# Final normalization: ten sequences added to the output by accumulating transfers, six by VectorE, and no barrier ahead of it

## The reference

```python
x = x + _L1_xattn_ref(_layernorm(x, axis=-1), ctx_1024)        # "x3" in the kernel
x = x + _L1_ffn_ref(_layernorm(x, axis=-1), ...)
# and the end of _L1_ffn_ref, whose argument z is the normed x3:
out = jnp.einsum('bted,bte->btd', y, combine)                  # top-2 of 8 experts
return _layer_norm(z + out, gamma, beta)
# so the result is  x3 + (norm(z + out) * gamma + beta)
```

## Time and profile before

| | |
|---|---|
| median of 3 runs | 1369.33 us (1367.33 to 1369.45) |
| the profiled execution | 1379.14 us |
| its span | 1377.3 us |
| TensorE busy | 1145.9 us, 83% of the span |
| VectorE busy | 938.2 us, 68% |
| ScalarE busy | 799.8 us, 58% |
| GpSimd busy | 650.4 us, 47% |
| moved by transfers | 162.79 MB, mean 118 GB/s |

### The profile page before, as it was taken

One profiled execution on the slowest core, in us unless ns is written; L12 is line 12 of the kernel. 1 busy time (PEld: TensorE's weight loads), 2 busy tenths in 40 slices (PEclk: granted clock), 3 DMA queues, 4 the chain that ended last, 5 costly groups with the idle time before them and its releaser, 6 DMA issues.

```text
span 1377.3 us, 24047 instructions
## 1 busy us (share of the span) xinstructions
PE 1145.9 (83%) x8296; PEld 1052.9 (76%) x8296; DVE 938.2 (68%) x2066; ACT 799.8 (58%) x1579; POOL 650.4 (47%) x581
## 2 busy tenths in 40 slices
PE   3889899898859999999948560999999999999920
PEld 2688778787648888888837450999999999999920
DVE  6667877876436666666347564678878788787848
ACT  3745666552325565555436520777787877778724
POOL 3434443333235666665424664354554544545347
PEclk8559998899979999999978775899999999999965
DMA  6543333211065666666369990233332333333256
GB/s 224 167 164 112 137 122 120 108 54 39 24 209 166 176 175 174 176 172 180 48 200 266 229 194 11 54 59 52 56 55 52 59 52 55 55 52 59 39 158 223
DMA packets 142313, 162.79 MB, mean 118 GB/s; under 512 B 29457, under 2 KB 122897, under 8 KB 140145
## 3 DMA queue, kind: packets, MB, share of 16 engines
q1 hardware_dynamic: 113120, 124.97, 29.8%
q0 software_dynamic: 27968, 35.48, 15.5%
q10 hardware_dynamic: 1104, 0.82, 0.2%
HBM read 117.36 MB, written 43.86 MB: 117 GB/s over the span
## 4 chain that ended last, share of the span: by engine, by line
PE 62%; DVE 13%; DMA 7%; issue 7%; ACT 5%; POOL 4%; POOLq 1%; SPq 1%; ACTq 0%; DVEq 0%
PE quad L1929 15%; PE pb L1948 12%; PE quad L1191 11%; PE pb L1206 6%; PE pb L354 4%; PE quad L300 4%; DMA c3T<-in_ctxT 4%; PE pb L368 3%; POOL dSL L1803 2%; DVE Dm L522 1%; PE pb L266 1%; ACT Dm L838 1%; POOLq L2230 1%; PE pb L1176 1%; PE quad L1910 1%
## 5 line engine op out<-in xcount | busy, mean ns | idle before, releaser
L1993 DVE TENSOR_TENSOR wl<-W,wh 128x1024 fp32r<-128x1024 f32 x156 | 188.4, 1228 | 86.4 <-ACT gl L2068 57.6
L2100 POOL DMA_INDIRECT dOUT<-y,es x71 | 135.3, 1905 | 219.8 <-DVE y L2025 210.1
L1948 PE MATMUL pb<-wh,hh 128*128 128x256 f32 x568 | 164.0, 289 | 0.0
L1948 PE MATMUL pb<-wh,hl 128*128 128x256 f32 x568 | 160.5, 283 | 0.0
L1948 PE MATMUL pb<-wl,hh 128*128 128x256 f32 x568 | 160.5, 283 | 0.0
L1332 POOL DMA_INDIRECT dACC<-ye,idxJ x64 | 100.6, 1572 | 103.6 <-ACT ye L1295 54.4
L2042 ACT CAST wh<-W 128x1024 fp32r x117 | 121.9, 1049 | 41.0 <-issue 29.1
L2068 ACT ACTIVATE gl<-quad,b1c 128x256 f32<-128x256 f32 (+1 forms) x312 | 124.7, 450 | 20.0 <-PE quad L1929 18.7
L1929 PE MATMUL quad<-xh,wh 128*128 128x256 f32 (+1 forms) x624 | 126.1, 284 | 6.7 <-ACT hh L2073 5.2
L1929 PE MATMUL quad<-xh,wl 128*128 128x256 f32 (+1 forms) x624 | 125.6, 283 | 0.0
L1929 PE MATMUL quad<-xl,wh 128*128 128x256 f32 (+1 forms) x624 | 125.6, 283 | 0.0
(11 more groups left out here) (282 smaller groups left out, 3202.7 us busy)
## 6 DMA issues: line engine op xcount, KB each, us to landing
MB<-dM SPq DMA_DIRECT2D x16, 1024.0 KB, 5.7
W<-in_W SPq DMA_DIRECT2D x16, 1024.0 KB, 10.8
wraw<-in_Wg SPq DMA_DIRECT2D x16, 512.0 KB, 6.5
wraw<-in_Wu SPq DMA_DIRECT2D x16, 512.0 KB, 8.0
wraw<-in_Wd SPq DMA_DIRECT2D x16, 512.0 KB, 5.3
b2c<-in_b SPq DMA_DIRECT2D x39, 128.0 KB, 3.2
xp<-in_x SPq DMA_DIRECT2D x16, 256.0 KB, 5.5
cT<-in_ctxT SPq DMA_DIRECT2D x16, 256.0 KB, 5.2
```

The costliest lines, as they stand in the source:

```text
L1948: ins = pe.matmul(bank.t[:, 0:256], a_[s][:, c, 128 * tt:128 * tt + 128], b_[n % 3][:, 256 * c:256 * c + 256], start=half == 0 and m == 0, ...
L1993: v.tensor_tensor(w_dst(wl[n % 3], kind), w_src(expert(i), kind, half), w_dst(wh[n % 3], kind), ALU.subtract).then_inc(*v_t.up("w", n))
L2100: g.indirect_dma_start(out=dOUT[:, :], out_offset=bass.IndirectOffsetOnAxis(ap=es[i % 6][:, tt, 1:2].bitcast(U32), axis=0), in_=y1[i % 2][ ...
```

## The change

x3 is stored straight into the rows of the output, and `dX3` is gone. During stage 4, in visits 4 to 19, GpSimd adds beta to the output's rows, one sequence at a time, with an accumulating transfer from the broadcast tile `bet`; for this gamma and beta are loaded at the end of stage 3. The barrier between stages 4 and 5 is gone: SP waits for the last scatters (`sy_st`) before it loads z, and all other waits of stage 5 follow from its loads. Stage 5 works on pairs of sequences, 128 x 4 columns of statistics at once, all 16 z tiles stay in place, and there is no load of x for the first ten sequences: GpSimd adds their norm * gamma to the output's rows with accumulating transfers. For the last six SP loads the output's rows (x3 + beta), VectorE adds in place and SP stores. ScalarE may overwrite a tile of `nc_` (four pairs) when its accumulating transfer has landed.

```diff
@@ stage 3, SP
-                    sp.dma_start(by_chunk(dX3[pair_rows(j), :]), x2[j % 4][:, :, :]).then_inc(*x3_st[j % 4].up(j, by=16))
+                    sp.dma_start(by_chunk(out[pair_rows(j), :]), x2[j % 4][:, :, :]).then_inc(*x3_st[j % 4].up(j, by=16))
...
+            sp.dma_start(gam[:, :], to_all(A["gamma"], D)).then_inc(*ln_ld.up("g", by=16))
+            sp.dma_start(bet[:, :], to_all(A["beta"], D)).then_inc(*ln_ld.up("b", by=16))
+            for s in (w1_ld, w2_ld, ln_ld, *x3_st, *z_st):
@@ stage 4, GpSimd (the loads of gamma and beta leave SP's part)
                 if i + 3 < VISITS:
                     gather(i + 3)
+                if 0 <= i - 4 < B:
+                    g.dma_start(by_chunk(out[rows(i - 4), :]), bet[:, :].unsqueeze(1).to_broadcast([128, 2, D]), accum_op=ALU.add
+                                ).then_inc(*beta_st.up(i - 4, by=16))
...
             g.wait_ge(*sy_st.all())
+            g.wait_ge(*beta_st.all())
@@ stage 5, new
+        ADDED = 2 * (PAIRS - 3)
+            def stats(j):
+                s = fsm[j]
+                for c in range(4):
+                    if c % 2 == 0:
+                        v.wait_ge(*fz_ld[2 * j + c // 2].of())
+                    ins = v.bn_stats(s[:, c, 0:6], zc[j][:, c, :])
...
+            def scale(b):
+                n = nc_[b // 2 % 4][:, chunks(b), :]
                 v.wait_ge(*a_f.of("n", b))
+                v.tensor_tensor(n, n, gam[:, :].unsqueeze(1).to_broadcast([128, 2, D]), ALU.mult).then_inc(*v_f.up("g", b))
+                if b >= ADDED:
+                    v.wait_ge(*v_f.of("g", b))
+                    v.wait_ge(*fx_ld[(b - ADDED) // 2].all())
+                    v.tensor_tensor(n, n, xc[(b - ADDED) // 2][:, chunks(b), :], ALU.add).then_inc(*v_f.up("y", b))
+
+            for j in range(PAIRS + 1):
+                if j < PAIRS:
+                    stats(j)
+                if j == 1:
+                    v.wait_ge(*ln_ld.all())
+                if j:
+                    scale(2 * j - 2)
+                if j < PAIRS:
+                    shift(j)
+                if j:
+                    scale(2 * j - 1)
...
+        def act_stage5(a):
+            for j in range(PAIRS):
...
+                    if c % 2 == 0 and j >= 4:
+                        a.wait_ge(*out_ad[b % 8].of(b - 8))
...
+        def pool_stage5(g):
+            def add(b):
+                g.wait_ge(*v_f.of("g", b))
+                g.dma_start(by_chunk(out[rows(b), :]), nc_[b // 2 % 4][:, chunks(b), :], accum_op=ALU.add
+                            ).then_inc(*out_ad[b % 8].up(b, by=16))
+
+            for j in range(PAIRS):
+                s = fsm[j]
+                g.wait_ge(*v_f.of("v", j))
+                g.tensor_tensor(s[:, :, 8:9], s[:, :, 9:10], mhalf[:, :].unsqueeze(1).to_broadcast([128, 4, 1]), ALU.pow).then_inc(*g_f.up("r", j))
+                if 0 < j <= ADDED // 2:
+                    add(2 * j - 2)
+                    add(2 * j - 1)
...
+        def sp_stage5(sp):
+            sp.wait_ge(*sy_st.all())
             for b in range(B):
+                sp.dma_start(zc[b // 2][:, chunks(b), :], by_chunk(dOUT[rows(b), :])).then_inc(*fz_ld[b].up(by=16))
+            sp.wait_ge(*beta_st.all())
+            for b in range(ADDED, B):
+                sp.dma_start(xc[(b - ADDED) // 2][:, chunks(b), :], by_chunk(out[rows(b), :])).then_inc(*fx_ld[(b - ADDED) // 2].up(b, by=16))
+            for b in range(ADDED, B):
                 sp.wait_ge(*v_f.of("y", b))
+                sp.dma_start(by_chunk(out[rows(b), :]), nc_[b // 2 % 4][:, chunks(b), :]).then_inc(*out_st.up(b, by=16))
@@ the programs of all engines: a barrier after stages 1 to 3 only
-                if n < 4:
+                if n < 3:
                     end_of_stage(v, n + 1)
```

More of the change, by code:

```diff
@@ L2116, in sp_stage4 @@
                 sp.dma_start(b2c[i % 4][:, :], A["b2"][bass.ds(r, 1), :].to_broadcast([128, D])).then_inc(*b2_ld[i % 4].up(i, by=16))
-            sp.dma_start(gam[:, :], to_all(A["gamma"], D)).then_inc(*ln_ld.up("g", by=16))
-            sp.dma_start(bet[:, :], to_all(A["beta"], D)).then_inc(*ln_ld.up("b", by=16))
-            sp.wait_ge(*ln_ld.all())
         M7.st.close()
         M8 = Mem()
-        fsm = M8.ring("fsm", 4, [128, 2, 16])
-        zc = M8.ring("zc", 12, [128, 2, D])
-        xc = M8.ring("xc", 8, [128, 2, D])
@@ L2128, in build @@
[L2128 to L2132, removed]
+        fsm = M8.ring("fsm", PAIRS, [128, 4, 16])
+        zc = M8.ring("zc", PAIRS, [128, 4, D])
+        nc_ = M8.ring("nc", 4, [128, 4, D])
+        xc = M8.ring("xc", 3, [128, 4, D])
+        ADDED = 2 * (PAIRS - 3)
+        fz_ld, fx_ld = ring("moe_loaded", B), ring("x3_loaded", 3)
+        out_ad, out_st = ring("out_added", 8), sig("out_stored")
@@ L2133, in build @@
         v_f, a_f, g_f = sig("dve_final"), sig("act_final"), sig("pool_final")
-        def x3_of(b):
-            return xc[b % 8]
         def dve_stage5(v):
[L2140 to L2149, removed]
-                    ins = v.bn_aggr(s[:, c, 6:8], s[:, c, 0:6])
[L2151 to L2157, removed]
+            def stats(j):
[4 more added lines that the diff above has]
+                    ins = v.bn_stats(s[:, c, 0:6], zc[j][:, c, :])
+                ins.then_inc(*v_f.up("s", j))
+                v.wait_ge(*v_f.of("s", j))
+                for c in range(4):
+                    ins = v.bn_aggr(s[:, c, 6:8], s[:, c, 0:6])
+                ins.then_inc(*v_f.up("a", j))
+                v.wait_ge(*v_f.of("a", j))
+                v.tensor_scalar(s[:, :, 9:10], s[:, :, 7:8], EPS, None, ALU.add).then_inc(*v_f.up("v", j))
@@ L2158, in shift @@
+            def shift(j):
+                s = fsm[j]
+                v.wait_ge(*g_f.of("r", j))
                 v.scalar_tensor_tensor(out=s[:, :, 10:11], in0=s[:, :, 6:7], scalar=-1.0, in1=s[:, :, 8:9],
-                                       op0=ALU.mult, op1=ALU.mult).then_inc(*v_f.up("b", b))
+                                       op0=ALU.mult, op1=ALU.mult).then_inc(*v_f.up("b", j))
             def scale(b):
+                n = nc_[b // 2 % 4][:, chunks(b), :]
                 v.wait_ge(*a_f.of("n", b))
-                v.tensor_tensor(nc_[b % 4][:, :, :], nc_[b % 4][:, :, :], gam[:, :].unsqueeze(1).to_broadcast([128, 2, D]),
-                                ALU.mult).then_inc(*v_f.up("g", b))
@@ L2166, in total @@
[L2166 to L2181, removed]
@@ L2184, in act_stage5 @@
-        def act_stage5(a):
-            for b in range(B):
[L2186 to L2202, removed]
@@ new lines, in act_stage5 @@
+        def act_stage5(a):
+            for j in range(PAIRS):
+                s = fsm[j]
+                a.wait_ge(*v_f.of("b", j))
+                for c in range(4):
+                    b = 2 * j + c // 2
+                    if c % 2 == 0 and j >= 4:
+                        a.wait_ge(*out_ad[b % 8].of(b - 8))
+                    ins = a.activation(nc_[j % 4][:, c, :], zc[j][:, c, :], ACT.Identity, scale=s[:, c, 8:9], bias=s[:, c, 10:11])
+                    if c % 2:
+                        ins.then_inc(*a_f.up("n", b))
@@ L2219, in sp_stage5 @@
+        def sp_stage5(sp):
+            sp.wait_ge(*sy_st.all())
+            for b in range(B):
+                sp.dma_start(zc[b // 2][:, chunks(b), :], by_chunk(dOUT[rows(b), :])).then_inc(*fz_ld[b].up(by=16))
[3 more added lines that the diff above has]
+            for b in range(ADDED, B):
                 sp.wait_ge(*v_f.of("y", b))
-                sp.dma_start(by_chunk(out[rows(b), :]), yc[b % 4][:, :, :]).then_inc(*out_st[b % 4].up(b, by=16))
@@ L2221, in sp_stage5 @@
-            for s in out_st:
+                sp.dma_start(by_chunk(out[rows(b), :]), nc_[b // 2 % 4][:, chunks(b), :]).then_inc(*out_st.up(b, by=16))
+            for s in (*out_ad, out_st):
                 sp.wait_ge(*s.all())
@@ L2235, in tensor_program @@
                 stage(pe)
-                end_of_stage(pe, n + 1)
+                if n < 3:
+                    end_of_stage(pe, n + 1)
         def vector_program(v):
```

5 lines of the change are left out of this document (2 added, 3 removed).

## The result

The changed kernel runs in 1364.9 us (median of 19 runs), the kernel before in 1372.9 us (also 19): the ratio is 0.9941, 95% interval 0.9927 to 0.9955, so 8.1 us faster (6.2 to 10.0). Forecast were 6.7 us. The 19 runs of before scatter from 1367.3 to 1379.5, more widely than the three of the first table.

A forecast was written before the change was run, and what follows sets the result against it. The bound was taken as VectorE's order in the last stage, behind a start waiting for barrier and first loads. Terms gave -8.6 us, less 1.9 for GpSimd's issues: 1369.3 - 6.7 = 1362.6 us, range 1357.5 to 1370.5.

The forecast's parts named there:

- Barrier: Seam between stages four and five: SP issues its first load without waiting for GpSimd's drain, -4.4 us.
- First loads: Start of stage five: all z go first, so the second z lands after 4.6 us, not 6.35.
- Pitch: Stage five, pairs without x: 4.43 us each, with VectorE waiting for the same pair's power; five take 22.2 us.
- Pairs with x: Stage five, three pairs with x on VectorE: 5.5 us each for two, 2.7 for the last.
- GpSimd's issue: Stage five, ten accumulating transfers: issuing one takes a = 1.55 us, stretching five pitches to 4.81, adding 1.9 us.
- the threshold of 1.36: Stage five: issue time a above which GpSimd's cycle is longer than 4.43 us and each of five pitches grows.
- the cycle of 1.71 + 2a: GpSimd's time per pair in stage five: power 1.01, signal 0.1, two issues of a plus 0.30 gap each.
- Rival 1: Dearer issues make GpSimd pace stage five: +3.7 us at 2.59, +8.8 at 3.1; chances 7 and 7 in 100.
- The two ends: Extremes of issue time in stage five: a = 0.96 leaves -8.6 us, a = 3.1 gives +8.8.
- Landing: Last stage's additions: 256 rows take 1.95 us of all DMA engines; ten end near 1357, covered by 10 us.
- Rival 2: Additions land slowly in the last stage: one after another at 7.4 us each, +32 us; 10 in 100.
- Stage four: Sixteen beta transfers in stage four hide in GpSimd's waits for y, costing nothing; rival 0 to 16 us, 8 in 100.

The follow-up runs named there:

- e1: The changed kernel with the barrier ahead of the last stage put back; ratio to the kernel before 0.9955 (0.9935 to 0.9974).
- e2: The kernel before with only the last barrier replaced by SP's wait for the scatters; ratio to the kernel before 0.9977 (0.9956 to 0.9998).
- e4: The changed kernel with both scales ahead of the shift in VectorE's order; ratio to the kernel before 0.9916 (0.9890 to 0.9943).
- e5: The changed kernel with VectorE one pair further ahead and GpSimd's adds one iteration later; ratio to the kernel before 0.9890 (0.9859 to 0.9921).
- e8: The changed kernel with GpSimd's ten last-stage transfers storing instead of accumulating; ratio to the kernel before 0.9913 (0.9884 to 0.9942).
- e10: The changed kernel with fourteen sequences added by accumulating transfers and two by VectorE; ratio to the kernel before 0.9984, one run each.
- e9: The changed kernel with sixteen more beta transfers, in visits 20 to 35 of stage four; ratio to the kernel before 0.9942, one run each.

## Why the prediction was right

**Barrier, -4.4.** Right, by e1 (5.4 us put back) and e2 (4.3 taken out of the old kernel).

**First loads.** The forecast gain came and was larger by 1.2 us. Eps of the first pair was due 5.9 us after the first load and came after 4.7, because the second z landed 3.5 us after the first load, when VectorE wanted it, and not 4.6. How much of this is the order of loads is not shown: with the old order the second z came after 6.4 us (before) or 4.3 (e2).

**Pitch.** 4.43 was forecast, 4.22 measured. The stall was placed rightly and nearly to its size: from eps to shift 1.69 (1345.92 to 1347.61), forecast 1.70, with a power of 1.39, forecast 1.36. What was off is VectorE's own work, 1.84 for statistics and aggregation instead of 2.02. e4 and e5 show that this stall is the pace.

**Pairs with x.** 4.95 instead of 5.5: power and add did not queue on each other, the shift came after 1.69 us as before.

**GpSimd's issue.** The step most in doubt. a = 1.55 was taken, 1.23 measured (1.38 for the beta transfers), and GpSimd still waited 0.41 us in a pitch, so the 1.9 us charged for it were not owed. That it stayed below the threshold of 1.36 proves little, since the cycle of 1.71 + 2a was mis-set in two places that nearly cancel: it has the power at 1.01, where the forecast's own pitch has 1.36, and a gap of 0.30 ahead of each issue, where the trace has none that is GpSimd's own. With 1.36 for the power the threshold would have been 1.18, and 1.23 would have paced the stage; e5, with a round of 3.2 us, shows that it doesn't. Rival 1 needed 2.22 and falls. The two ends were both off as prices of this form: 0.96 is too little for 256 accumulating rows and 3.1 far too much. The page "DMA: Bandwidth & Descriptors" of the Trainium skill ("Anatomy of one DMA — SWDGE (gpsimd) path") calls descriptor generation small and says that many descriptors can be emitted before their cost shows. The 0.75 us of e8's stores of 256 rows fit that; for additions a cost of rows shows at once (0.98 us for 128, 1.31 for 256), yet one that is too small to matter here.

**Landing.** 1.95 us was the price for 256 rows, 1.34 is measured (e5). The cover was real in the changed kernel: the last addition lands at 1354.3, 8.7 us ahead of the last store, where the forecast had 10 to the end. Rival 2 falls. What the forecast does not have at all is GpSimd's closing drain behind the additions; in the changed kernel it is covered, in e10 it ends the program.

**Stage four.** The issues are covered, as forecast: GpSimd's wait shrank by them, and e9 with twice as many is no longer. The forecast named a longer stage four as a sign of being wrong, and the profile has it 1.4 us longer; kernels with the same sixteen transfers differ by 2.5, so this neither shows a price nor excludes one.

**Sum.** On the profile the terms that I overcharged are 1.2 (loads), 5 x (4.81 - 4.22) = 3.0 (pitch and issue) and 1.1 (two pitches with x), 5.3 in all; the gap and the tail shrank by 4.4 + 7.4 = 11.8, and 6.7 + 5.3 is 12.0. The runs show 8.1 (6.2 to 10.0), so the forecast fits them better than its terms fit the profile, and that is luck in part. What takes 2 to 6 us of these 12 away in the runs is only partly known. The tail of before was a long one: with the same stage 5 e2 has 48.5 and not 49.9, which takes off 1.4. Up to 1.4 may be a longer stage four. The start of stage four scatters too (866.2 to 871.4 within the series of e1 to e4, 860.0 to 863.1 in that of e5 to e8). The rest is open.

## What to carry to other kernels

In a stage in which one engine's hand-written order sets the pace, halving the number of steps also shortens the distance between a result and its use: look for the wait that this opens (here 0.93 us in 4.22), and give the order back its lookahead (e5, another 5 us). An accumulating transfer takes a read and an add off the engines for about 1.2 us of GpSimd per 256 rows of 1 KB, but it occupies the DMA engines about twice as long as a plain one (196 against 384 GB/s), and GpSimd's closing drain stands behind the last one; use it for the early part of a stage and not for the end. A barrier between stages costs GpSimd's drain besides the last landing (4.4 us here), and one semaphore wait on the queue that starts the next stage replaces it.

## What the runs showed of the hardware

- GpSimd's drain behind indirect transfers that had already landed took 4.4 us at the last barrier of before and 5.4 in e1. Its closing drain took 5.6 us in the changed kernel and 9.7 in e10, where it ended 3.3 us after the last addition had landed (1363.1) and ended the program.
- Issuing a plain transfer from GpSimd took 0.75 us for 256 rows stored, 1.2 to 1.4 for 256 rows accumulated, 0.98 for 128 rows accumulated; in e5 the second of two additions started 0.76 us after the first. Ten stores of 256 KB were 800 packets (e8), ten additions of the same size 2720; an indirect one of 128 rows takes 0.96 and 1.55.
- Accumulating transfers that had piled up ran at 196 GB/s (e5, 1344 to 1349), where loads and stores ran at 384.
- A power of four columns on GpSimd took 1.05 us beside an idle VectorE and 1.39 beside its multiplication of two tiles. The page "SBUF — State Buffer" of the Trainium skill, section "Who interferes with whom", says that a VectorE instruction with two SBUF inputs and a GpSimd instruction that reads SBUF shut each other out; the 0.34 us go the same way. But the additions of x, also of two tiles, ran inside such a power (1350.94 to 1351.63 in one from 1350.41 to 1351.80) without being longer than their 0.69, so the rule does not cover all of it.
